# Causal attention of one layer: from loops over key heads to one written-out order of steps, rows from last to first

## The reference

```python
B, S, D = (2, 256, 256); H, KV, HD = (16, 4, 128)      # the kernel runs it with S = 1024
def attention(x, wq, wk, wv, wo):
    q = (x @ wq).reshape(b, s, H, HD)
    k = (x @ wk).reshape(b, s, KV, HD)
    v = (x @ wv).reshape(b, s, KV, HD)
    q = apply_rope(q, cos, sin)
    k = apply_rope(k, cos, sin)
    k = jnp.repeat(k, rep, axis=2)
    v = jnp.repeat(v, rep, axis=2)
    scores = jnp.einsum('bqhd,bkhd->bhqk', q, k) / np.sqrt(HD)
    scores = jnp.where(causal[None, None], scores, jnp.finfo(scores.dtype).min)
    probs = jax.nn.softmax(scores, axis=-1)
    out = jnp.einsum('bhqk,bkhd->bqhd', probs, v).reshape(b, s, H * HD)
    return out @ wo
attn_out = attention(rmsnorm(hidden_states, norm1_w), wq, wk, wv, wo)
h = hidden_states + attn_out
```

## Time and profile before

| | us |
|---|---|
| median of 3 runs | 2849.14 (2845.28 to 2851.73) |
| the profiled execution, its own time | 2845.13 |
| span of its trace | 2843.0 |
| attn2, from its first instruction to its last addition into hs | 1484.4 to 2532.7 |

### The profile page before, as it was taken

One profiled execution on the slowest core, in us unless ns is written; L12 is line 12 of the kernel. 1 busy time (PEld: TensorE's weight loads), 2 busy tenths in 40 slices (PEclk: granted clock), 3 DMA queues, 4 the chain that ended last, 5 costly groups with the idle time before them and its releaser, 6 DMA issues. The chain is left out here.

```text
span 2843.0 us, 38075 instructions
## 1 busy us (share of the span) xinstructions
PE 2450.6 (86%) x12622; PEld 1899.0 (67%) x12622; DVE 1613.1 (57%) x2795; ACT 1133.2 (40%) x1919; POOL 1107.8 (39%) x659
## 2 busy tenths in 40 slices
PE   6949989968999959969973989999799989976997
PEld 2339989955777648847853777777577777753554
DVE  6558878863222244434437667676566667674332
ACT  3547766711111124314421545445354545441121
POOL 0448777702232214303413343443344344412443
PEclk9969999988999979969976999999889999998999
DMA  6262171246112120000000000000000000026222
GB/s 238 102 273 54 60 282 67 82 131 201 33 31 35 25 89 1 1 1 1 1 28 31 12 12 0 12 0 12 1 12 12 0 12 0 1 81 194 44 44 62
DMA packets 101188, 161.86 MB, mean 57 GB/s; under 512 B 30324, under 2 KB 69878, under 8 KB 98808
## 3 DMA queue, kind: packets, MB, share of 16 engines
q1 hardware_dynamic: 86040, 138.93, 13.8%
q0 software_dynamic: 14976, 20.78, 4.3%
HBM read 111.62 MB, written 50.22 MB: 57 GB/s over the span
## 5 line engine op out<-in xcount | busy, mean ns | idle before, releaser
L1801 POOL TENSOR_TENSOR a_e<-a_e,a_rc 128x128 f32<-128x128 f32 (+5 forms) x192 | 220.2, 1147 | 373.6 <-DVE a_rc L1733 373.3
L669 POOL TENSOR_TENSOR mb_dbx<-mb_ud,mb_bb 128x1024 f32<-128x1024 f32 x128 | 301.6, 2361 | 101.9 <-DVE mb_h L529 81.6
L529 DVE TENSOR_TENSOR_SCAN mb_h<-ps,mb_dbx 128x1024 f32<-128x1024 f32 x128 | 292.1, 2287 | 62.6 <-ACT ps L639 49.8
L1845 ACT ACTIVATE a_e<-ps,a_nb 128x128 f32<-128x128 f32 (+7 forms) x256 | 189.9, 742 | 231.8 <-DVE a_nb L1746 230.6
L962 POOL DMA_INDIRECT e_acc<-e_hid,e_ids x78 | 123.6, 1585 | 371.7 <-DVE e_hid L1258 363.5
L766 PE MATMUL ps<-mb_dg,mb_hts 128*128 128x128 f32 x2048 | 257.0, 280 | 3.5 <-DVE mb_xz L518 3.5
L1745 DVE TENSOR_REDUCE a_mx<-ps 128x1 f32<-128x128 f32 (+7 forms) x256 | 193.7, 757 | 98.5 <-PE ps L1928 97.9
L766 PEld LDWEIGHTS ps<-mb_dg,mb_hts 128*128 128x128 f32 x2048 | 245.9, 197 | 5.2 <-DVE mb_xz L518 5.2
L1858 ACT ACTIVATE a_eThi<-ps 128x512 fp32r<-128x512 f32 x288 | 169.7, 595 | 168.5 <-PE ps L1961 167.1
L1244 DVE COPY e_work<-ps 128x256 f32<-128x256 f32 x78 | 33.1, 424 | 357.1 <-PE ps L1077 357.1
L1552 POOL TENSOR_TENSOR a_elo<-a_e,a_ehi 128x1024 fp32r<-128x1024 f32 x48 | 120.5, 2511 | 272.5 <-ACT a_ehi L1476 272.5
(11 more groups left out here) (331 smaller groups left out, 5604.1 us busy)
## 6 DMA issues: line engine op xcount, KB each, us to landing
mb_bb<-mb_db_rows SPq DMA_DIRECT2D x16, 1024.0 KB, 12.9
mb_ddiag<-mb_dg SPq DMA_DIRECT2D x1, 8192.0 KB, 22.4
mb_dg<-mb_ddiag SPq DMA_DIRECT2D x8, 1024.0 KB, 20.6
e_wg<-in_g SPq DMA_DIRECT2D x8, 688.0 KB, 10.7
e_wu<-in_u SPq DMA_DIRECT2D x8, 688.0 KB, 11.0
e_wd<-in_d SPq DMA_DIRECT2D x8, 640.0 KB, 10.8
mb_dxa<-mb_bb SPq DMA_DIRECT2D x8, 512.0 KB, 2.6
mb_dz<-mb_xz SPq DMA_DIRECT2D x8, 512.0 KB, 2.9
```

Source lines behind the costliest of these rows:

```text
L529: dve.tensor_tensor_scan(h[:, at % 2, :], pair(at % 2), dbx[:, at % 2, :], 0.0, ALU.mult, ALU.add).then_inc(s_h, 1)
L669: pool.tensor_tensor(dbx[:, at % 2, :], ud[:, kk % 2, 0, :], bb[:, n, :], ALU.mult).then_inc(s_dbx, 1)
L1801: pool.tensor_tensor(e[:, i % 2, h, 0:(i + 1) * P], e[:, i % 2, h, 0:(i + 1) * P], rc[:, q:q + 1].to_broadcast([P, (i + 1) * P]), ALU.mult ...
L1845: act.activation(e[:, i % 2, h, 0:(i + 1) * P], pair(n % 2, (i + 1) * P), ACT.Exp, bias=nb[:, q:q + 1], scale=SCALE, accum_out=sm[:, q:q + ...
```

## The change

Only `attn2` changes. There are no loops; one list `schedule()` for all 8 units is walked by every engine. Rows of a unit come in the order 7 to 0. Row 6's and row 0's scores lie beside row 7's blocks, row 5's beside row 6's, those of rows 4 and 1 beside row 5's, of rows 3 and 2 beside row 4's. The next unit's projections, the key first, lie beside rows 3, 2 and 1; its values come between its own first scores. The layer norm and the second norm of batch 1 are cut into small steps ("chores") on DVE beside the first 26 turns of unit 0, with two square roots on ACT; batch 1's rows are scaled beside unit 3 and transposed there in two `flip` steps. x is written to DRAM at the start of the stage and read back once the last heads are rotated; its SBUF holds rotation buffers and batch 1's scaled rows meanwhile. e holds the rows at other places (PLACE, GONE).

```diff
+        KEY, NPROJ = 0, REP + 1
+        def schedule():
+            todo, waiting = [], []
+            put = lambda *t: todo.append(t)
+            def value(u, i, j):
+                if j == min(i, 1) and (u, i) != (0, TB - 1):
+                    put("out", u if i < TB - 1 else u - 1, (i + 1) % TB, 0)
+                put("value", u, i, j)
+            def turn(u, i, j):
+                put("turn", u, i, j)
+                waiting.append((u, i, j))
+                if len(waiting) > 2:
+                    value(*waiting.pop(0))
...
+            ahead_proj = {(3, 0): 0, (3, 2): 1, (2, 0): 2, (2, 2): 3, (1, 1): 4}
+            put("flip", 0, 0, 0)
+            put("flip", 0, 1, 0)
+            for n in range(NPROJ):
+                put("project", 0, n, 0)
+            for u in range(U):
+                put("score", u, 7, 0)
+                put("score", u, 7, 1)
+                while waiting:
+                    value(*waiting.pop(0))
+                put("score", u, 7, 2)
+                put("values", u, 0, 0)
+                put("score", u, 7, 3)
+                for i in range(TB - 1, -1, -1):
+                    for j in range(i + 1):
...
+                        if u + 1 < U and (i, j) in ahead_proj:
+                            put("project", u + 1, ahead_proj[i, j], 0)
+                        turn(u, i, j)
+                        if (u + 1) % KV == 0 and u + 1 < U and (i, j) in ((5, 3), (4, 1)):
+                            put("flip", (u + 1) // KV, i == 4, 0)
...
         @block.sync
+            sp.dma_start(d_x.rearrange("(j p) d -> p j d", p=P), x[:, :, :]).then_inc(s["xout"], 16)
+            for u in range(U):
...
+                if u == 0:
+                    for dst, src in loads:
+                        sp.dma_start(dst, src).then_inc(s["in"], 16)
+            sp.wait_ge(s["rope"], U * REP)
+            sp.wait_ge(s["rope_k"], U)
+            sp.wait_ge(s["xout"], 16)
+            sp.dma_start(x[:, :, :], d_x.rearrange("(j p) d -> p j d", p=P)).then_inc(s["xin"], 16)
...
         @block.vector        (steps turn and project)
+                elif what == "turn":
+                    if (i, h) == (TB - 1, 0):
+                        extra = chores(u)
+                    if unturned:
+                        low(*unturned.pop(0))
+                    unturned.append((u, i, h))
...
+                elif what == "project":
+                    if unturned:
+                        low(*unturned.pop(0))
+                    dve.wait_ge(s["unit"], done[what, u, i, h])
+                    if i >= 3:
+                        dve.wait_ge(s["rope"], heads(u, i - 2))
+                    elif i == 2:
+                        dve.wait_ge(s["rope_k"], u + 1)
+                    elif u > 0:
+                        dve.wait_ge(s["rope"], heads(u - 1, REP - 1 + i))
...                  (the three passes of the rotation)
+                    if i == 1:
+                        dve.wait_ge(s["high"], u * NPROJ + 1)
+                        dve.tensor_tensor(kT[LO][:, :], a[:, KEY, :], kT[HI][:, :].bitcast(F32), ALU.subtract).then_inc(s["rope_k"], 1)
...
         @block.gpsimd
+                elif what == "project":
+                    add(u, i)
+                    if i >= 2:
+                        low(u, i - 1)
+                    if i == REP:
+                        low(u, i)
...
         @block.scalar
+            for n, (what, u, i, h) in enumerate(todo):
+                if what == "turn":
+                    k = turned[u, i, h]
+                    act.wait_ge(s["tp"], k + 1)
+                    act.activation(eT[HI][:, k % 3, :], ps[:, bank[what, u, i, h], :], ACT.Copy).then_inc(s["eT"], 1)
+                    if u == 0 and (i, h) == (7, 5):
+                        root(1, 3)
+                    if u == 0 and (i, h) == (4, 3):
+                        root(1, 4)
+                while held and what in ("turn", "score", "value", "values", "project", "out"):
+                    exponential(*held.pop(0))
+                if what == "score":
+                    held.append((u, i, h))
...
+                elif what == "value" and h == i:
+                    act.wait_ge(s["o"], rows[u, i] + 1)
...                  (ao)
+                if what == "project":
+                    unhigh.append((u, i))
+                if unhigh and what in ("turn", "project", "score") and (what != "project" or len(unhigh) > 1):
+                    if what == "turn" or len(unhigh) > 1 or what == "score":
+                        high(*unhigh.pop(0))
```

More of the change, by code:

```diff
@@ L1594, in attn2 @@
         block = ctx.enter_context(nc.Block())
[L1595 to L1650, removed]
@@ new lines, in attn2 @@
+        todo = schedule()
+        unit = {t: n for n, t in enumerate(t for t in todo if t[0] in ("score", "project", "values", "flip"))}
+        unit_at = {n: t for t, n in unit.items()}
+        done = {t: c + 1 for c, t in enumerate(t for t in unit if t[0] != "flip")}
+        scored = {t[1:]: n for n, t in enumerate(t for t in todo if t[0] == "score")}
+        turned = {t[1:]: n for n, t in enumerate(t for t in todo if t[0] == "turn")}
+        outs = {t[1:3]: n for n, t in enumerate(t for t in todo if t[0] == "out")}
@@ new lines, in attn2, with pair, normed @@
+        rows = {ui: n for n, ui in enumerate(outs)}
+        ring = [t for t in todo if t[0] in ("turn", "out")]
+        ring_at = {t: r for r, t in enumerate(ring)}
+        bank = {t: (4, 5, 7)[r % 3] for t, r in ring_at.items()}
+        def pair(n, w=L, p=slice(0, P)):
+            return flat(ps[p, 2 * (n % 2):2 * (n % 2) + 2, :])[:, 0:w]
+        def normed(u, i):
+            return [scored[u, i, h] for h in range(REP)]
+        by_pool = {n: c + 1 for c, n in enumerate(n for (u, i, h), n in scored.items() if h < REP - 1)}
@@ new lines, in centred, with modulated, scaled @@
+            def centred(j0, n):
+                for j in range(j0, j0 + n):
+                    own.mark(dve.tensor_scalar(hs[:, j, :], x[:, j, :], mean[:, j:j + 1], rstd[:, j:j + 1], ALU.subtract, ALU.mult))
+            def modulated(b, j0, n, which, op):
+                own.wait()
+                h = hs[:, j0:j0 + n, :]
+                own(dve.tensor_tensor(h, h, over(mod[:, b, which * D:(which + 1) * D], n), op))
+            def scaled(b, j0, n):
+                dst = rows_in(b)
+                if b > 0 and j0 == 0:
+                    dve.wait_ge(s["rope"], b * KV * REP)
+                    dve.wait_ge(s["rope_k"], b * KV)
+                    dve.wait_ge(s["xout"], 16)
+                for j in range(j0, j0 + n):
+                    c = b * TB + j
+                    ins = dve.scalar_tensor_tensor(dst[:, j, :], hs[:, c, :], rstd[:, c:c + 1], nwb[:, :], ALU.mult, ALU.mult)
+                if j0 + n == TB:
+                    ins.then_inc(s["xn"], 1)
@@ new lines, in exponential @@
+            def exponential(u, i, h):
+                n = unit["score", u, i, h]
+                q = i * REP + h
+                act.wait_ge(s["nb"], scored[u, i, h] + 1)
+                for row in GONE[i]:
+                    earlier = u - 1 if i in EARLY else u
+                    if h == 0 and earlier >= 0:
+                        act.wait_ge(s["tp"], turned[earlier, row, row] + 1)
+                act.activation(probs(i, h), pair(n, (i + 1) * P), ACT.Exp, bias=nb[:, q:q + 1],
+                               scale=SCALE, accum_out=sm[:, q:q + 1]).then_inc(s["e"], 1)
@@ new lines, in ring_free @@
+            def ring_free(t):
+                r = ring_at[t]
+                if r >= 3:
+                    what, u, i, j = ring[r - 3]
+                    if what == "turn":
+                        pe.wait_ge(s["eTlow"], turned[u, i, j] + 1)
+                    else:
+                        pe.wait_ge(s["hs"], outs[u, i] + 1)
+            for token in todo:
+                what, u, i, j = token
+                if token in unit:
+                    n = unit[token]
+                    unit_free(n)
+                    o = n % 2
+                if what == "flip":
+                    if i == 0:
+                        pe.wait_ge(s["xn"], u + 1)
+                    for c in range(TB):
+                        tr = pe.transpose(ps[:, 2 * o + c // 4, (c % 4) * P:(c % 4 + 1) * P],
+                                          rows_in(u)[:, c, int(i) * P:(int(i) + 1) * P], ident[:, :])
@@ L1987 @@
+    g.norms += 4
 class Shared:
```

533 lines of the change are left out of this document (265 added, 268 removed).

## The result

The changed kernel takes 2952.4 us (median of 4, 2951.7 to 2954.1) against 2850.4 for the kernel before, runs side by side: ratio 1.036, 95% interval 1.0342 to 1.0378. Slower, by 102 us. The prediction was 2940, range 2870 to 3025. The profiled execution took 2951.9, its span 2950.0.

A forecast was written before the change was run, and what follows sets the result against it. PE sets the pace mid-unit, so gains lie where it waits. Start -12.5, periods +108, change of batch -6, first stretch +17, last unit -17 and chores +6 sum to +95.5 on 2845.1: 2941, called 2940, range 2870 to 3025.

The forecast's parts named there:

- case A: Unit tails: `high` on ACT spaces rotations 8.6 us apart, PE stalls 25.7 us; total 2940, chance 0.70.
- a term of its own (4): Each ordinary unit: 4 us added for lost PE clock, between nothing and 10.
- The period: Each of 6 ordinary units takes 138.1 us against 120.1, +18.0 each, +108 in all.
- Start: Before the first projections: batch 1's half of the norm goes, -12.5 us; x's copy to DRAM stays hidden.
- Change of batch: Between batches: 143 us in place of 149.5, -6, with no stage without cover left.
- Chores: Unit 0: norm steps on DVE and table loads for two square roots cost +6 us, bounds 0 and 15.
- First stretch: Unit 0's first projection to its first turn: 52 us, +17 against before; POOL's order spaces later rotations 8.5.
- Last unit: Behind the last unit's first turn: 75.2 us of PE work plus 7 of stalls, 82 against 99.6, so -17.
- Rival B: Unit tails: the clock stays low through them, at least +7 us per unit, total some 3020; chance 0.10.
- Rival C: Unit tails: `high` on ACT waits for nothing, only POOL's order remains; period 121.6, total 2825, chance 0.09.
- S: Stretch from the key's projection to row 7's first turn; forecast 69.5 us in the likeliest case.
- Rival D: Unit tails: projections are hidden fully, first turn at 48 us, period 112.6, total 2762; chance 0.07.

The follow-up runs named there:

- the last kernel: Changed kernel with `high` later, POOL's lo earlier, ao, third and fourth scores reordered, unit 0's values early: 2763.8 us, 0.9705 of the kernel before.
- the kernel with just that: Changed kernel with `high` at the third turn behind its projection, POOL's order kept: 2851.3 us, ratio 1.0016 to the kernel before.
- the next kernel: Kernel with the fourth score ahead of the values, plus the third score between value (1,1) and its out: 2769.4 us in one run.

## Why the prediction was right, point by point

- **The tail (case A).** Rotations forecast at 3.1, 11.7, 20.3, 28.9, 37.5, measured 3.0, 11.3, 20.8, 29.4, 38.0. Value (1,0) forecast at 45.4, measured 45.9. First turn forecast at 69.5, measured 73.1. In it PE's waits are 19.6 us, not 25.7, but its own work takes longer than the 43.8 at the full clock: in a window of 73 us over the tail it is busy 53.4 at a granted clock of 0.88. The clock's loss lies in this stretch, for which I had a term of its own (4). Moving `high` alone took 101 us away, and moving it the other way in the kernel before put 107 on: shown from both sides.
- **The period.** Forecast 138.1 (57.6+7+69.5+4), measured 136.4: the rest of a unit is 63.3, where I had 64.6. Two of its terms were off and offset each other: PE works 60.4 us in the 63 below, for which I had 57.6, and is idle 2.6, for which I had 7. Six times 16.3 are +98, forecast +108.

```profile
1857.00:1920.00 63.00, 60.36 (x348) 50.11 (x349) 44.38 (x115) 36.87 (x84) 24.45 (x23) 0.95 0.05 14
```

- **Start.** -13.2 (43.5 to 30.3), forecast -12.5. x's copy to DRAM ahead of the loads raised the DMA share there from 0.27 to 0.69 and held ACT's first rounding of weights 7.1 us, which nothing on the way to the first projection waited for: hidden, as forecast.
- **Change of batch.** 143.7 for 149.5: -6, as forecast.
- **Chores.** 7.5 more in unit 0's period than in an ordinary one (143.9 less 136.4), forecast 6; the run without them says 8.2. In the last kernel, where the tails are short, unit 0 takes 10.3 more (121.7 and 111.4).
- **First stretch, mis-sized.** Forecast 52 us to the first turn, measured 59.9, so +25 in place of +17. The rotations came as forecast (4.4, 8.1, 13.2, 21.8, 30.3), and the second score at 34.1. "In unit 0 nothing stands in the tail's way" fails a little: `high` of the last head and a table load stand ahead of the first exponential, whose maximum was ready at 1552.1, and the third score waits for that. It starts at 40.1, where "end at 47" implies 38.9. No run moved this `high`.

```profile
1553.17 1.06 ACT L1945 ACTIVATE a_qThi<-a_e 128x1024 fp32r<-128x1024 f32 x1 [7.50 <-POOL a_e L1887]
1554.25 1.28 ACT L1939 ACT_TABLE_LOAD   x1
1555.55 1.11 ACT L1939 ACTIVATE a_e<-ps,a_nb 128x1024 f32<-128x1024 f32 x1
```

  The step that failed is the next: "the third, values, and fourth score end at 47" takes them at the full clock, 8.1 us. They took some 17, without a wait, and end at 57. Before them PE had worked only 6.1 of 14.6 us; during the values the granted clock was 0.50, and they alone took 10.0 us for 5.3:

```profile
1542.20:1556.80 14.60, 6.12 (x14) 3.94 (x14) 5.07 (x6) 4.60 (x5) 10.70 (x5) 0.62 0.00 0
1560.00:1570.00 10.00, 10.00 (x49) 10.00 (x48) 1.28 (x2) 1.20 (x2) 1.66 (x1) 0.50 0.00 0
```

- **Last unit, mis-sized.** 91.3 us behind its first turn, forecast 82: -8 in place of -17. PE is idle 7.3 of them, as forecast (7). The term that failed is its own work, "75.2": it is 84.0 at a clock of 0.97, and the last kernel has 82.2 at 1.00. By distances between starts the 36 blocks take some 45 us, not 41.0, and a ninth `out`, of the unit before, was left out. I had set a sum of parts (82) against a measured stretch (99.6), in which the kernel before has just as much of what the sum leaves out: 92.0 of work and 7.5 idle.

```profile
2360.80:2450.30 89.50, 82.18 (x467) 66.41 (x465) 56.16 (x137) 45.57 (x100) 21.84 (x21) 1.00 0.00 1
```

- **Sum.** 98+7.5-6+25-8-13.2 = +103.3 against a measured +102.9 for the stage (1151.2 us for 1048.3). The two misses add 17, and the overestimate of the periods takes 10 back. The mechanism and the size of the tail were right; that the total came within 0.4% is partly luck.
- **Rival B** (clock low through the tails) fell: 0.88 in the window of a tail, which lies near the 0.82 of the earlier trace rows that I had set against it. The Trainium skill (TensorE: Matmul & The Clock Gate, Part 1) has it that the throttled state is the default and activity releases it. In this tail, where PE was busy 53.4 of 73 us with waits of up to 7.2 us, the rows show 0.88, so the low level was not the rule through it. (The 0.82 of the earlier trace rows belongs to 22.9 busy of 35.0 us, more than the "half-busy" of the prediction.)
- **Rival C** was the right mechanism for what comes second: I gave S 57 and a period of 121.6 if only POOL's order remained, and the kernel with just that showed 59.1 and 121.9. Its total (2851) was above my 2825, mostly by unit 0's first stretch (60.1, not 52) and the last unit, the two terms above. **Rival D**'s S 48 and period 112.6, total 2762, is what the mended kernel reached, with other lists than the change has: 48.2, 111.3, 2764.
- **The table loads.** The first root behind exponentials costs two loads of 1.28, with work starting directly at their end:

```profile
1588.68 1.28 ACT L1922 ACT_TABLE_LOAD   x1
1589.97 0.21 ACT L1922 ACTIVATE a_a_n_sd<-a_a_n_var 128x8 f32<-128x8 f32 x1
1590.20 1.28 ACT L1939 ACT_TABLE_LOAD   x1
1591.49 0.37 ACT L1939 ACTIVATE a_e<-ps,a_nb 128x128 f32<-128x128 f32 x1
```

The drain of some 1.38 that the Trainium skill (ScalarE: Activation LUTs, What ACT_TABLE_LOAD costs) adds does not show here: 1588.68 to 1589.97 is the load alone, and the copy ahead of it ended at 1588.66.

## What to carry to other kernels

When one list of steps is walked by several in-order engines, a step's place in the list is right only for the engine that starts it. For each engine that comes later in the chain, ask when its input will be there and what stands behind it in the meantime, and give it a token of its own, late enough that its input is there and early enough for its consumer. Then follow the circle round: here hi, ao and lo, which had nothing to do with the rotated head, carried its delay to the next rotation, and moving the lo away without asking who waits for it made a longer circle.

## What was not expected of the hardware

- Fewer waits came with more clock, but not one for one. Two units of one execution with the same instructions and the same idle time of PE (9.4 and 9.5 us) took 115.7 us at 1.00 and 120.4 at 0.96; what decided between them no run here shows. In the next kernel PE is idle 5.6 us in such a unit, all five ran at 1.00, and their mean fell from 118.4 to 111.3: of the 7 us, some 4 are waits and some 3 the clock.
- The reverse holds too: with `high` early the kernel before ran its units at 0.87 in place of 0.95, and lost 17 us per unit, 8 of them idle time and 9 longer work of PE.
